# Perceiver with two layers: the second cross attention's second pass in rounds of three half tiles

## What is computed

```python
def _L1_xattn_ref(query, key, value, Wq, bq, Wk, bk, Wv, bv, Wo, bo):
    H, D = 16, 16
    q = (query @ Wq + bq).reshape(B, Nq, 16, 16).transpose(0, 2, 1, 3)
    k = (key @ Wk + bk).reshape(B, Nk, 16, 16).transpose(0, 2, 1, 3)
    v = (value @ Wv + bv).reshape(B, Nk, 16, 16).transpose(0, 2, 1, 3)
    attn = jnp.einsum('bhqd,bhkd->bhqk', q, k) * 16 ** (-0.5)
    attn = jax.nn.softmax(attn, axis=-1)
    out = jnp.einsum('bhqk,bhkd->bhqd', attn, v)
    return out.transpose(0, 2, 1, 3).reshape(B, Nq, 256) @ Wo + bo
x = x + _L1_xattn_ref(_layernorm(x, axis=-1), ctx, ctx, ...)
```

## Time and profile before

| what | value |
|---|---|
| median of 3 runs | 1196.99 us (1196.62 to 1197.66) |
| the profiled execution's own time | 1198.74 us |
| span of the profile | 1196.9 us |
| TensorE busy with matmuls | 1147.4 us, 96% |
| VectorE busy | 670.1 us, 56% |
| ScalarE busy | 670.7 us, 56% |
| GpSimdE busy | 212.8 us, 18% |
| mean granted TensorE clock | 0.981 |
| second pass of the second layer | about 905 to 1120 us of the span |

### The profile page before, as it was taken

How to read it: one execution, slowest core, us unless ns; L and a number is a source line. 1 busy time by engine, 2 the same in 40 slices (tenths; PEclk the granted TensorE clock), 3 DMA queues, 4 the chain that set the end, 5 groups by cost and what they waited for, 6 DMA issues and landing times.

```text
span 1196.9 us, 29049 instructions
## 1 busy us (share of the span) xinstructions
PE 1147.4 (96%) x10066; PEld 938.4 (78%) x10066; DVE 670.1 (56%) x1138; ACT 670.7 (56%) x1092; POOL 212.8 (18%) x312
## 2 busy tenths in 40 slices
PE   6999899999999999999777999999999999999998
PEld 5887788888888888878664888888887888888874
DVE  5999543444444344343744788888885444444443
ACT  1888334433333443434021588888877888889520
POOL 0000100000000000000102577778740110000310
PEclk8999999999999999999879999999998999999999
DMA  3444711001100100100634466767665895555380
GB/s 136 135 138 131 307 41 35 26 26 30 31 26 26 35 26 26 35 26 18 237 119 168 158 229 224 231 219 229 222 227 182 282 305 196 182 180 184 133 312 5
DMA packets 62027, 163.97 MB, mean 137 GB/s; under 512 B 6640, under 2 KB 7088, under 8 KB 56304
## 3 DMA queue, kind: packets, MB, share of 16 engines
q1 hardware_dynamic: 53360, 118.54, 29.9%
q0 software_dynamic: 8640, 45.05, 10.4%
HBM read 124.87 MB, written 38.67 MB: 137 GB/s over the span
## 4 chain that ended last, share of the span: by engine, by line
PE 90%; DVE 7%; issue 1%; ACT 1%; DMA 0%; DVEq 0%; ACTq 0%
PE ps L650 62%; PE ps L899 8%; PE ps L838 8%; PE ps L692 2%; PE ps L638 1%; PE ps L703 1%; PE ps L707 1%; PE ps L704 1%; PE ps L706 1%; PE ps L705 1%; PE ps L1197 1%; PE ps L1034 1%; PE ps L1175 1%; PE ps L1056 0%; DVE probs L1488 0%
## 5 line engine op out<-in xcount | busy, mean ns | idle before, releaser
L1413 DVE TENSOR_TENSOR wide<-wide,probs 128x1024 f32<-128x1024 f32 x97 | 118.9, 1226 | 246.0 <-ACT probs L500 246.0
L1345 DVE TENSOR_TENSOR wide<-ps,wide 128x512 f32<-128x512 f32 (+1 forms) x196 | 186.9, 954 | 30.8 <-PE ps L650 26.2
L511 ACT ACTIVATE probs<-ps 128x1024 f32<-128x1024 f32 x196 | 190.3, 1023 | 22.2 <-PE ps L650 22.0
L483 ACT CAST wide<-ps 128x512 bf16<-128x512 f32 x294 | 162.3, 587 | 29.2 <-PE ps L650 24.5
L500 ACT ACTIVATE probs<-ps 128x512 f32<-128x512 f32 x196 | 117.1, 598 | 104.8 <-PE ps L650 104.8
L650 PE MATMUL ps<-q_ha,t_ha 128*128 128x512 f32 x392 | 157.2, 401 | 3.8 <-DVE q_le L1273 3.8
L1350 DVE TENSOR_TENSOR wide<-wide 128x512 bf16<-128x512 bf16 (+1 forms) x196 | 108.5, 554 | 13.0 <-ACT wide L483 2.8
L650 PE MATMUL ps<-q_ab,q_hk 128*128 128x512 f32 x392 | 107.1, 394 | 0.0
L899 PE MATMUL ps<-probs,v_sb 128*32 128x128 f32 x3136 | 106.8, 277 | 0.1
L1401 DVE COPY v_sb<-wide 128x256 f32<-128x256 f32 x98 | 28.8, 294 | 119.8 <-PE ps L899 119.6
L650 PEld LDWEIGHTS ps<-q_ha,t_ha 128*128 128x128 f32 x392 | 75.5, 193 | 21.1 <-DVE q_le L1273 4.3
(11 more groups left out here) (385 smaller groups left out, 2321.7 us busy)
## 6 DMA issues: line engine op xcount, KB each, us to landing
raw<-ctx_in SPq DMA_DIRECT2D x147, 256.0 KB, 2.6
k_mem<-q_hk SPq DMA_DIRECT2D x49, 512.0 KB, 3.0
v_mem<-probs SPq DMA_DIRECT2D x49, 256.0 KB, 3.5
wide<-v_mem SPq DMA_DIRECT2D x49, 256.0 KB, 4.2
ring<-ex_in POOLq DMA_DIRECT2D x8, 1152.0 KB, 12.5
q_le<-k_mem SPq DMA_DIRECT2D x17, 512.0 KB, 4.2
q_ab<-k_mem SPq DMA_DIRECT2D x16, 512.0 KB, 4.4
q_hk<-k_mem SPq DMA_DIRECT2D x16, 512.0 KB, 4.4
```

What stands on the lines that cost most here:

```text
L483: act.copy(half16[:, c:c + 512], ps[:, back_bank(layer, q) + u, :]).then_inc(sem(f"half{layer}"), 1)
L511: act.activation(probs[:, at:at + 1024], ps[:, bank:bank + 2, :].rearrange("p b n -> p (b n)"), ACT.Exp).then_inc(sem("exp1"), 1)
L1345: dve.tensor_tensor(r, ps[:, b:b + half // 512, :].rearrange("p b n -> p (b n)"), r, ALU.max)\
L1413: dve.tensor_tensor(run[:, 0:1024], run[:, 0:1024], e, ALU.add).then_inc(sem("lsum"), 1)
```

## The change

TensorE's order in the second pass now goes by halves, in rounds of three: three halves of scores, m = 3q to 3q+2, then the products of the three halves before them. The exponentials get six buffers instead of four (four in `probs`, two in the part `scr` of `wide`, which the second pass did not use), so ScalarE's wait for products is on half n-6 instead of n-4. The three pairs of banks stay, taken by the half's number. The number of matmuls and exponentials, their shapes, and the programs of VectorE, SyncE and GpSimdE stay the same. The first 12 halves are written out (the first round has no products), a loop runs 15 times over four rounds, and the last four halves are written out.

```diff
--- before.py
+++ after.py
@@ -197,6 +197,7 @@
         e_keep = [probs[:, i * 1024:(i + 1) * 1024] for i in range(2 * GT)]
 
         stage = probs[:, 0:2048]
+        e_half = [probs[:, i * 1024:(i + 1) * 1024] for i in range(4)] + [scr[:, i * 1024:(i + 1) * 1024] for i in range(2)]
         v_in = [run[:, i * 512:(i + 1) * 512] for i in range(KSLOTS)]
         q_all = probs[:, 2048:3072]
         block = stack.enter_context(nc.Block())
@@ -249,9 +250,11 @@
                     body(i, slot, False)
             body(GROUPS // KSLOTS, 0, False, True)
 
-        def pair_bank(slot, j, w):
-
-            return s_pair[(4 * slot + 2 * j + w) % 3]
+        HALVES = 4 * KSLOTS
+
+        def pair_bank(m):
+
+            return s_pair[m % 3]
 
         def groups(eng, body):
 
@@ -500,16 +503,15 @@
                         act.activation(e_keep[GT * slot + j][:, u * 512:(u + 1) * 512], ps[:, s_bank[j][u], :],
                                        ACT.Exp).then_inc(sem("exp0"), 1)
 
-            def exps1(t, slot, j, first):
-
-                for w in range(2):
-                    n = 2 * t + w
-                    act.wait_ge(sem("s2_1"), n + 1)
-                    if not first:
-                        act.wait_ge(sem("pv1"), n - 3)
-                    at, bank = j * 2048 + w * 1024, pair_bank(slot, j, w)
-                    act.activation(probs[:, at:at + 1024], ps[:, bank:bank + 2, :].rearrange("p b n -> p (b n)"),
-                                   ACT.Exp).then_inc(sem("exp1"), 1)
+            def exps1(i, m, first):
+
+                n = HALVES * i + m
+                act.wait_ge(sem("s2_1"), n + 1)
+                if not (first and m < 6):
+                    act.wait_ge(sem("pv1"), n - 5)
+                bank = pair_bank(m)
+                act.activation(e_half[m % 6], ps[:, bank:bank + 2, :].rearrange("p b n -> p (b n)"),
+                               ACT.Exp).then_inc(sem("exp1"), 1)
 
             def keep_keys(g, slot, first):
 
@@ -574,8 +576,8 @@
                 act.wait_ge(sem("v_out1"), kv_count(1, GROUPS - 2))
 
                 def body(i, slot, first, last=False):
-                    for j in range(GT):
-                        exps1((KSLOTS * i + slot) * GT + j, slot, j, first and slot == 0)
+                    for m in range(4 * slot, 4 * slot + 4):
+                        exps1(i, m, first)
                 rounds(act, body)
 
             def cross(layer):
@@ -872,54 +874,61 @@
                         step(2 * i + 1, 1, False)
                     back(GROUPS - 1, 0, stop=True)
 
-                def pairs1(i, slot, j, new=False):
-
-                    if j == 0:
+                def scores_half(i, m, new=False):
+
+                    slot, j, w = m // 4, m // 2 % 2, m % 2
+                    if m % 4 == 0:
                         pe.wait_ge(sem("k_again"), KSLOTS * i + slot + 1)
-                    t = (KSLOTS * i + slot) * GT + j
-                    for w in range(2):
-                        n = 2 * t + w
-                        if not (new and n < 3):
-                            pe.wait_ge(sem("exp1"), n - 2)
-                        bank = pair_bank(slot, j, w)
-                        for u in range(4 * w, 4 * w + 4):
-                            last = mm(ps[:, bank + u % 4 // 2, (u % 2) * 256:(u % 2 + 1) * 256],
-                                      kp[slot][:, u * GK + j * P:u * GK + (j + 1) * P], q_ha[:, u * 256:(u + 1) * 256], 0, 1)
-                        last.then_inc(sem("s2_1"), 1)
-
-                def products1(t, j, start, stop):
-
-                    for w in range(2):
-                        pe.wait_ge(sem("exp1"), 2 * t + w + 1)
-                        if w == 0:
-                            pe.wait_ge(sem("v_sb1"), t + 1)
-                        for u in (2 * w, 2 * w + 1):
-                            for k in range(4):
-                                h = 4 * u + k
-                                last = pe.matmul(ps[32 * k:32 * k + 32, 4, u * P:(u + 1) * P],
-                                                 v_sb[j][:, h * 32:(h + 1) * 32],
-                                                 probs[:, j * 2048 + h * P:j * 2048 + (h + 1) * P],
-                                                 start=(start and u == 0), stop=stop, skip_group_check=True)
-                        last.then_inc(sem("pv1"), 1)
+                    if not (new and m < 3):
+                        pe.wait_ge(sem("exp1"), HALVES * i + m - 2)
+                    bank = pair_bank(m)
+                    for u in range(4 * w, 4 * w + 4):
+                        last = mm(ps[:, bank + u % 4 // 2, (u % 2) * 256:(u % 2 + 1) * 256],
+                                  kp[slot][:, u * GK + j * P:u * GK + (j + 1) * P], q_ha[:, u * 256:(u + 1) * 256], 0, 1)
+                    last.then_inc(sem("s2_1"), 1)
+
+                def products_half(i, m, start=False, stop=False):
+
+                    j, w = m // 2 % 2, m % 2
+                    pe.wait_ge(sem("exp1"), HALVES * i + m + 1)
+                    if w == 0:
+                        pe.wait_ge(sem("v_sb1"), HALVES // 2 * i + m // 2 + 1)
+                    for u in (2 * w, 2 * w + 1):
+                        for k in range(4):
+                            h = 4 * u + k
+                            at = (h - 8 * w) * P
+                            last = pe.matmul(ps[32 * k:32 * k + 32, 4, u * P:(u + 1) * P], v_sb[j][:, h * 32:(h + 1) * 32],
+                                             e_half[m % 6][:, at:at + P], start=(start and u == 0), stop=stop,
+                                             skip_group_check=True)
+                    last.then_inc(sem("pv1"), 1)
 
                 def second1():
 
                     keep_warm(12, 3)
                     pe.wait_ge(sem("q_lo"), 2)
                     pe.wait_ge(sem("max_row"), 32)
-                    pairs1(0, 0, 0, True)
-
-                    def body(i, slot, first, last=False):
-                        t = (KSLOTS * i + slot) * GT
-                        pairs1(i, slot, 1, first)
-                        products1(t, 0, first and slot == 0, False)
-                        if not last:
-                            if slot < KSLOTS - 1:
-                                pairs1(i, slot + 1, 0, first)
-                            else:
-                                pairs1(i + 1, 0, 0)
-                        products1(t + 1, 1, False, last)
-                    rounds(pe, body)
+                    def threes(i, new=False):
+
+                        for q in range(HALVES // 3):
+                            for m in range(3 * q, 3 * q + 3):
+                                scores_half(i, m, new)
+                            for m in range(3 * q, 3 * q + 3):
+                                if q > 0:
+                                    products_half(i, m - 3, new and m == 3)
+                                elif not new:
+                                    products_half(i - 1, HALVES - 3 + m)
+
+                    threes(0, True)
+                    with pe.Fori(1, GROUPS // KSLOTS) as i:
+                        threes(i)
+                    end = GROUPS // KSLOTS
+                    for m in range(3):
+                        scores_half(end, m)
+                    for m in range(HALVES - 3, HALVES):
+                        products_half(end - 1, m)
+                    scores_half(end, 3)
+                    for m in range(4):
+                        products_half(end, m, stop=True)
 
                 (second0, second1)[layer]()
```

## The result

The changed kernel takes 1201.78 us (median of 8 runs, 1200.23 to 1202.79); the kernel before, run beside it, 1198.24 us (8 runs, 1196.62 to 1200.07). The ratio is 1.0027, with a 95% interval of 1.0017 to 1.0038: 3.2 us more, 2.0 to 4.5. Forecast were 2.0 us more and 1199.0 us, on the 1196.99 us of the first three runs, with "same" at 0.46 and "slower by over 0.2%" at 0.42. The sign and the rough size are right. Of the 2.8 us between forecast and measured time 1.25 are the other median of the kernel before, and 1.5 lie in the difference. The ratio itself falls in "slower", but its interval reaches over the border of 1.002, so the runs do not separate the two cases.

A forecast was written before the change was run, and what follows sets the result against it. TensorE's own stream was taken to bound the second pass. Turns -10.5, key-cast waits +12.8 and the end -0.4 summed to +1.9, taken as +2 us: 1199.0 us for the median, range 1195.5 to 1203.

The forecast's parts named there:

- same: Whole kernel time within 0.2% (2.4 us) of no change, 1194.6 to 1199.4 us; chance 0.46.
- Item 1: TensorE's second pass: 32 fewer pairs of turns between scores and products, 0.33 us each, -10.5 us.
- items 1 and 6: Turns saved in the pass (-10.5 us) plus start and end of the pass (0 and -0.4 us).
- Item 2: ScalarE's exponentials in rounds of three: they fit the 3.08 us round and nothing waits, 0 us.
- Item 3: TensorE's scores wait for VectorE's key cast in 31 groups, late by 0.44 or 0.39 us: +12.8 us.
- The wake-up of 0.11: From cast end to TensorE's weight load: 0.11 us taken; bounds on the wait +11.3 (at 0.06) to +16.2 us.
- Items 4 and 5: Value-tile buffers and key loads in the second pass: enough slack, no new waits, 0 us each.
- A: Rival: the key cast comes earlier, so its wait does not fall on TensorE; 1186.1 us, chance 0.11.
- B: Rival: the wait for the key cast is longer, or key loads slip; 1202.4 or 1202 us, chance 0.16.
- D: Rival: a third of the turn price reappears inside longer blocks, saving 7 us, not 10.5; 1202.5 us, chance 0.05.
- C: Rival: TensorE's granted clock drops after the new waits; three drops would give 1208 us, chance 0.04.

The follow-up runs named there:

- e1: Changed kernel with VectorE's key cast moved ahead of both value copies of its group: 1187.83 us, 0.9918 of the kernel before.
- e2: Kernel before with only the key cast moved ahead of the value copies: 1198.62 us, 0.9999 of the kernel before.
- e5: e1 with rounds of one half instead of three, same lag of three halves: 1229.95 us, 1.0265 of the kernel before.
- e4: Changed kernel with one more value copy, read by nothing, ahead of the copy and the cast: 1207.52 us, 1.0077 of the kernel before.
- e0: The changed kernel run again, unaltered, beside the experiments: 1201.90 us, 1.0025 of the kernel before.
- e6: Changed kernel with the cast early only for groups 1 and 2 mod 3, else behind the first value copy: 1187.94 us, 0.9918 of before.

## Why the prediction was right, point by point

- **What bounds the pass.** TensorE's own stream: shown by e1 against e2 (the same place of the cast, TensorE's new order against its old one: 10 us less) and e2 against before (another order of VectorE alone: nothing gained).
- **Item 1, turns.** 0.33 us a pair forecast; 0.35 measured between before and e1, 0.33 between e1 and e5. 32 pairs at 0.35 are -11.2 us, where -10.5 was forecast. The round of 3.08 is 3.07. In e1's trace the pass, from the first score load to the last product's end, takes 205.3 us, against 215.4 before; with its one late load taken out (1.1) the change is -11.2, forecast -10.9 for items 1 and 6.
- **Item 2, ScalarE.** In the steady part nothing waits for it: in e1 its exponentials of a round run without a gap and TensorE waits for none of them.
- **Item 3, the new wait.** 31 waits, on q_ab and q_hk, none on q_le, 0.40 and 0.36 us of idle loads and 0.45 and 0.41 of longer rounds, forecast 0.44 and 0.39. The wake-up of 0.11 that the choice between the bounds hung on is 0.12 (1040.75 to 1040.87). By the lengths of the rounds that is 15 x 0.45 + 16 x 0.41 = 13.3 us, where 12.8 was forecast. So the pass grew by 2.1 us (217.5 against 215.4), forecast 1.9. The sum came out closer than its terms: both were some 0.6 us larger than forecast, with opposite signs. (Two of its readings are 0.01 us off, with no effect: by the rows the copy and cast take 1.55 us, not 1.54, and three exponentials 2.76, not 2.77.)
- **Items 4 and 5.** In the changed kernel no cast waited for its load and TensorE for no value copy, as forecast. The slack was real but not large: in e1, where the casts come two product halves earlier, the late loads do reach TensorE, once in the one trace and twice in the other.
- **Rivals.** A (no wait, 1186.1) did not happen by the change, but e1 made it happen: 1187.8. B, longer waits, and D, turns cheaper to save, are refuted by the sizes above, and not by the time: 1201.78 us lies nearer to their 1202.4 and 1202.5 than to the forecast's 1199.0, while the 3.2 us over the kernel before lie nearer to the forecast's 2.0 than to their 5.4 and 5.5. C, the clock: granted 1.00 all through the stretch with its waits, two in every 13.1 us and 4 us apart, and in e4 with waits of 0.6. By the rule on short idle times that the prediction cited from the Trainium skill (TensorE: Matmul & The Clock Gate, A second HAM failure mode: psum-queue depth-cycling) the clock should have come and gone; the traces do not agree for waits of this length.
- **The rule that only turns count.** TensorEngine Tiling (Array Packing), Key Properties, of the Trainium skill says that a change of tiling mode drains the array. The nearly equal price per turn in e1 and e5 (0.35 and 0.33 us) agrees, though no run shows that the drain is what is paid for; by itself the rule gave 1186, since it says nothing of who else lives on the order.
- **What stays open.** The timed runs put the change at 3.2 and 3.0 us, the profiled executions of before and after at 2.2. The intervals take in both. The part outside the pass, which the edits leave alone, differs too: in the ten traces of this case the pass begins between 903.6 and 907.1 us, and 76.1 to 78.1 us follow it. Together that is more than the effect, so the growth of the pass itself, 2.1 us, is the firmer figure, and where the other microsecond of the timed runs comes from is open. The border between "same" and "slower", 2.4 us, lies inside the interval, so the runs say little on how well 0.46 and 0.42 were chosen.

## What to carry to other kernels

A reordering that saves a fixed price per switch is worth the number of switches saved, which can be read from single starts at the switch. Before it is made, look for work of other engines that is released by one of the moved pieces and needed by another: the distance between the two, in time, is what the reordering changes, and a chain of copy and cast that had 4 us of cover had 1.8 afterwards. Often the chain need not hang on that release at all: here the cast depended on nothing that the copy's wait guards, and moving it turned +3 us into -10.

## What was not expected of the hardware

The granted clock at the start of the pass differs between executions of one and the same kernel. The changed kernel's first profile, then its second (e0), in two windows of 4 us (the third number from the right is the clock):

```profile
904.00:908.00 4.00, 3.23 (x16) 2.94 (x16) 1.61 (x3) 3.24 (x4) 0.00 (x0) 0.56 0.10 37
908.00:912.00 4.00, 4.00 (x58) 3.56 (x57) 0.11 (x1) 3.65 (x4) 0.00 (x0) 0.59 0.49 161
```

```profile
904.00:908.00 4.00, 2.09 (x18) 1.93 (x18) 3.91 (x5) 0.06 (x1) 0.00 (x0) 1.00 0.64 198
908.00:912.00 4.00, 2.21 (x15) 1.66 (x13) 0.85 (x2) 3.99 (x5) 0.00 (x0) 1.00 0.00 1
```

In the first it is 0.56 and 0.59, in the second 1.00, though TensorE is idle for two microseconds ahead of the pass in both. The pass took 217.5 us in the one and 216.4 in the other: a difference of 1.1 us that no edit made, half the size of what was being measured. It arises in the first rounds: from the first score matmul to the start of the fifth block of scores it is 14.75 us in the one (903.92 to 918.67), 13.68 in the other (907.13 to 920.81). In three of the ten traces of this case (e0, e4, e6) the clock stays at 1.00 there, in seven it falls to 0.50 for about 7 us, and in all ten the weight loads had been idle for 2.1 us just before. Two VectorE copies, one behind the other, cost 0.21 us and not 0.29 (e4). And from the cast's end to the weight load, with the wait carried by a register instruction of TensorE, passed 0.12 us, where a matmul that carries the wait itself took 0.06; these are two places in the kernels, and no run changed the carrier alone.
